# A transposed-input copy moved from VectorE to ScalarE, and a transpose round moved inside the down projection, in an eight-core transformer layer

## The chip, the cores and the metric

The kernel runs on all 8 cores of one Trainium2 chip. Each core takes one batch element of the input and runs the same program on it; the cores exchange nothing. The metric is the device time of the slowest core, in microseconds (us). The engines are called PE (TensorE), DVE (VectorE), ACT (ScalarE), POOL (GpSimd) and SP (SyncE).

## The reference

One layer with normalisation after each half, for x of 8 x 4096 x 1024, with 16 heads of 64 and a hidden width of 4096:

```python
x = _layernorm(x + attention(x, w_qkv, w_out))      # causal softmax attention
x = _layernorm(x + ffn(x, w_up, w_down))
def _ternary_linear(x, w):
    alpha = jnp.mean(jnp.abs(w))
    w_t = jnp.sign(w) * (jnp.abs(w) > 0.5 * alpha).astype(w.dtype)
    w_q = w + jax.lax.stop_gradient(w_t - w)
    rms = jnp.sqrt(jnp.sum(x * x, axis=-1, keepdims=True)) / jnp.sqrt(jnp.asarray(d, x.dtype))
    return jnp.einsum('bsd,fd->bsf', x / (rms + EPS), w_q)
# ffn: h = gelu(_ternary_linear(x, w_up)); return _ternary_linear(h, w_down)
```

## The kernel before

A core's 4096 rows of x are 32 tiles of 128 rows (NT = 32). The program has three blocks, with a barrier of all engines between them.

Phase 1 (function `phase1`) makes K and V for all tiles and sums |w_up| and |w_down| for the two thresholds. For each tile i it loads the tile as bf16 into `xb1` (POOL issues the DMA), transposes it in eight 128x128 pieces on PE into a PSUM bank (`trp` or `trq` in turn), and copies the bank to `xTs` in SBUF; that copy is the mark `xTe`. PE then transposes K of the tile before (`k_trans(i - 1)`, into `tru` or `trv`, evicted to `KT` by DVE) and runs 32 matmuls of 128x512 into `kvp`, which have to wait for `xTe`. ACT evicts the K half to `kbuf` (mark `ke`) and the V half to `VS` (mark `ve`), and then runs two passes of Abs with a sum over a 128x1024 chunk of the weights (`sqA`, mark `aact`), fed by SP's loads into `wr1`. DVE squares and reduces K for a bound of the softmax. Each engine runs its instructions strictly in the order in which the program emits them, so on ACT the two Abs passes that are emitted at the end of tile i - 1 stand ahead of everything that is emitted for tile i.

Phase 2 is the attention with the output projection and the first normalisation; x1 goes to HBM (`x1spill`). The diff doesn't touch it.

Phase 3 makes ternary weights, transposes them on PE (`tern_chunk`), and then runs the feed-forward part over the 32 tiles. For tile i, `up_trans(i)` transposes x1 on PE into the PSUM bank `tra`; DVE copies it to `x1Ts` (mark `x1Te`); the load of `x1f` is issued on SP. `up_part(i)` is 64 matmuls in 8 groups with a Gelu on ACT behind each (mark `gel`). `down_part(i)` consists of four transposing rounds `hround(0..3)`, which bring the hidden values through `trb` (rounds 0 and 2, evicted by ACT) or `tra` (rounds 1 and 3, evicted by DVE) to `hTs`, and four rounds `dround(0..3)` of 16 matmuls each into `dwn`. A handwritten order holds the loop together: `up_trans(i + 2)`, `down_part(i)`, `up_part(i + 2)`. The bank `tra` is shared by `up_trans`, `hround(1)` and `hround(3)`: `state["tra"]` keeps the mark of the eviction that has to be over before PE writes it again.

Of the kernel before, what the change touches and what calls it, by code (L numbers as in the profile page):

```python
# [10 lines left out]
AF = mybir.ActivationFunctionType  # L11
# [7 lines left out]
NT = S // 128  # L19
# [99 lines left out]
def build_program():  # L119
# [25 lines left out]
    with ExitStack() as octx:  # L145
# [38 lines left out]
        with ExitStack() as ctx:  # L184
# [6 lines left out]
            xTs = sb("xTs", [128, 2, 8, 128], BF16)  # L191
# [18 lines left out]
            def phase1(E):  # L210
                t, v, a, g, y = E.t, E.v, E.a, E.g, E.y
# [34 lines left out]
                for i in range(NT):  # L246
                    if i >= 2:
                        g.wait(("xT", i - 2))
                    E.gdma(("xb", i), xb1[:, i % 2, :],
                           x_hbm[128 * i:128 * i + 128, :])  # L250
                    t.wait(("xb", i))
                    t.wait(("c", 6))
                    if i >= 2:
                        t.wait(("xTe", i - 2))
                    xtb = (trp_b, trq_b)[i % 2]
                    for c in range(8):
                        t.transpose(xtb[:, 128 * c:128 * c + 128],
                                    xb1[:, i % 2, 128 * c:128 * c + 128],
                                    idn[:])
                    t.mark(("xT", i))  # L260
                    v.wait(("xT", i))
                    if i >= 2:
                        v.wait(("kv", i - 2))
                    v.tensor_copy(xTs[:, i % 2],
                                  xtb[:, 0:1024].rearrange(
                                      "p (c n) -> p c n", n=128))
                    v.mark(("xTe", i))
                    if i >= 1:
                        k_trans(i - 1)
                    t.wait(("xTe", i))  # L270
                    t.wait(("wkv",))
                    for nb in range(4):
                        if nb == 0 and i >= 1:
                            t.wait(("ke", i - 1))
                        if nb == 2 and i >= 1:
                            t.wait(("ve", i - 1))
                        for c in range(8):
                            t.matmul(kvp[:, 512 * nb:512 * nb + 512],
                                     xTs[:, i % 2, c, :],
                                     wkv[:, c, 512 * nb:512 * nb + 512],  # L280
                                     start=(c == 0), stop=(c == 7))
                        if nb == 1:
                            t.mark(("kvK", i))
                    t.mark(("kv", i))
                    a.wait(("kvK", i))
                    if i >= 2:
                        a.wait(("ktr", i - 2))
                        a.wait(("knr", i - 2))
                    a.activation(kbuf[:, i % 2, :], kvp[:, 0:D], AF.Copy)
                    a.mark(("ke", i))  # L290
                    a.wait(("kv", i))
                    a.wait(("vs1",))
                    a.activation(VS[:, i, :, 0:64],
                                 kvp[:, D:2 * D].rearrange(
                                     "p (h e) -> p h e", e=64), AF.Copy)
                    a.mark(("ve", i))
                    for ii in ([i - 1] if i >= 1 else []) + \
                            ([i] if i == NT - 1 else []):
                        v.wait(("ve", ii))
                        v.scalar_tensor_tensor(sqK[:], kbuf[:, ii % 2, :],  # L300
                                               1.0, kbuf[:, ii % 2, :],
                                               ALU.mult, ALU.mult)
                        v.mark(("ksq", ii))
                        v.wait(("ksq", ii))
                        v.reduce_sum(sm16[:], sqK[:].rearrange(
                            "p (h e) -> p h e", e=64), axis=AX.X)
                        v.mark(("knr", ii))
                        v.wait(("knr", ii))
                        v.wait(("km0",))
                        v.tensor_max(kmax[:], kmax[:], sm16[:])  # L310
                        v.mark(("kmx", ii))
                    for r in (2 * i, 2 * i + 1):
                        if r >= 2:
                            y.wait(("aact", r - 2))
                        if r < 32:
                            src_ap = wup_hbm[128 * r:128 * r + 128, :]
                        else:
                            rr = r - 32
                            src_ap = wdn_hbm[
                                128 * (rr // 4):128 * (rr // 4) + 128,  # L320
                                1024 * (rr % 4):1024 * (rr % 4) + 1024]
                        E.ydma(("aw", r), wr1[:, r % 2, :], src_ap)
                        a.wait(("aw", r))
                        if r >= 1:
                            a.wait(("aact", r - 1))
                        acc = (aasU[:, r:r + 1] if r < 32
                               else aasD[:, r - 32:r - 31])
                        a.activation(sqA[:], wr1[:, r % 2, :], AF.Abs,
                                     accum_out=acc)
                        a.mark(("aact", r))  # L330
# [599 lines left out]
        with ExitStack() as ctx:  # L930
# [29 lines left out]
            def phase3(E):  # L960
# [115 lines left out]
                    for q in range(8):  # L1076
                        up_part_q(i, q)

                def down_part(i):
                    def hround(k):  # L1080
                        t.wait(("gel", i, 2 * k + 1))
                        bb = (trb_b, tra_b)[k % 2]
                        if k % 2 == 0:
                            if i >= 1 or k >= 2:
                                pk = (i, k - 2) if k >= 2 else (i - 1, 2)
                                t.wait(("hTe",) + pk)
                        else:
                            t.wait(state["tra"])
                        for u in range(8):
                            t.transpose(bb[:, 128 * u:128 * u + 128],  # L1090
                                        h_sb[:, i % 2,
                                             1024 * k + 128 * u:
                                             1024 * k + 128 * u + 128],
                                        idn[:])
                        t.mark(("hT", i, k))
                        ev = a if k % 2 == 0 else v
                        ev.wait(("hT", i, k))
                        ev_src = bb[:, 0:1024].rearrange(
                            "p (c n) -> p c n", n=128)
                        if k % 2 == 0:  # L1100
                            ev.activation(hTs[:, 8 * k:8 * k + 8, :],
                                          ev_src, AF.Copy)
                        else:
                            ev.tensor_copy(hTs[:, 8 * k:8 * k + 8, :],
                                           ev_src)
                        ev.mark(("hTe", i, k))
                        if k % 2 == 1:
                            state["tra"] = ("hTe", i, k)

                    def dround(k):  # L1110
                        if k == 0 and i >= 2:
                            t.wait(("y2", i - 2))
                        t.wait(("hTe", i, k))
                        t.wait(("wTe", 32 + 8 * k + 7))
                        for fc in range(8 * k, 8 * k + 8):
                            for nb in range(2):
                                t.matmul(
                                    dwn2[i % 2][:, 512 * nb:512 * nb + 512],
                                    hTs[:, fc, :],
                                    wdnT[:, fc, 512 * nb:512 * nb + 512],  # L1120
                                    start=(fc == 0), stop=(fc == 31))

                    hround(0)
                    hround(1)
                    dround(0)
                    hround(2)
                    dround(1)
                    hround(3)
# [85 lines left out]
                for i in range(NT):  # L1214
                    if i + 3 < NT:
                        issue_x1b(i + 3)
                    if i + 2 < NT:
                        up_trans(i + 2)
                    down_part(i)
                    if i + 2 < NT:  # L1220
                        up_part(i + 2)
                y.wait(("oD", NT - 2))
# [28 lines left out]
```

How the kernel before makes its waits and increments, by code:

```python
    def mark(self, key, inc=1):  # L42
        prog = self.prog
        if prog.planning:
            prog.ctr[self.name] += inc
            assert key not in prog.marks, f"dup mark {key}"
            prog.marks[key] = (self.name, prog.ctr[self.name])
        elif self.real is not None and inc:
            self.last.then_inc(prog.sems[self.name], inc)
# [1 line left out]
    def wait(self, key):  # L51
        prog = self.prog
        if prog.planning or key is None or self.real is None:
            return
        src, val = prog.marks[key]
        seen = prog.waited.get((self.name, src), 0)
        if val <= seen:
            return
        prog.waited[(self.name, src)] = val
        self.real.wait_ge(prog.sems[src], val)
# [18 lines left out]
    def _dma(self, eng, stream, key, out, in_):  # L79
        ring = DMA_STREAMS[stream]
        if self.planning:
            o = self.snum.get(stream, 0)
            self.snum[stream] = o + 1
            sname = f"q_{stream}{o % ring}"
            assert key not in self.marks, key
            self.marks[key] = (sname, 16 * (o // ring + 1))
        if eng.real is not None:
            ins = eng.real.dma_start(out, in_)
            object.__setattr__(eng, "last", ins)
            sname, _ = self.marks[key]
            ins.then_inc(self.sems[sname], 16)
```

## Time and profile before

| what | value |
|---|---|
| median of 3 runs | 3401.02 us (3397.51 to 3469.15) |
| the profiled execution | 3402.24 us |
| its slowest core (core 7), first to last instruction | 3400.7 us |
| spans of the 8 cores | 3377.3 to 3400.7 us |
| mean granted PE clock of core 7 | 0.830 of full speed |
| PE, DVE, ACT busy | 2650.6, 971.5, 1851.8 us |

In all views "idle before <-releaser" is the time for which the engine stood still ahead of a group, and what ended it. The granted clock is given as a share of full speed (2.4 GHz); it has two levels, 1.00 and 0.50, and a number between them is a mean over a stretch. Matmuls are pipelined and the ends of their rows are modelled, so a group of matmuls reads some tenths of a us too long, and the next group can begin before it ends.

### The profile page before, as it was taken

How to read it: one execution, taken by the hardware profiler on the slowest of the kernel's cores; microseconds unless marked ns; L12 is line 12 of the kernel's file. 1: busy time of each engine (PE TensorE's matmuls, PEld its weight loads, DVE VectorE, ACT ScalarE, POOL GpSimd, SP SyncE). 2: the span in 40 equal slices, each digit the busy share in tenths (PEclk: the TensorE clock that was granted, in tenths of full speed). 3: DMA queues.
4: the chain of work that ended last, by engine and by line, in shares of the span. 5: the costliest groups of instructions: out<-in, count | busy, mean ns of one | idle time of the engine just before them, and what ended most of it. 6: DMA issues, size and time to landing. Idle time of an engine off the chain costs nothing. (4 is left out here: it accounts for less than half of the span.)

```text
span 3400.7 us, 52712 instructions; the slowest of 8 cores (3377.3 to 3400.7 us)
## 1 busy us (share of the span) xinstructions
PE 2650.6 (78%) x19808; PEld 1322.4 (39%) x19808; DVE 971.5 (29%) x2483; ACT 1851.8 (54%) x2165; POOL 115.7 (3%) x231
## 2 busy tenths in 40 slices
PE   5996466777777777787777888343699999999998
PEld 2443222333333343344344444122344444444444
DVE  5443353443332323212311201544311111111111
ACT  2553122546576877877887886445434343334343
POOL 0000000000000000000000000000000000000000
PEclk9998676777787888967889655555799999999999
DMA  6666301010101101001000000443211111111111
GB/s 134 155 156 140 49 1 50 15 51 11 50 14 33 32 1 45 20 1 38 26 1 14 26 14 1 143 136 124 71 47 45 33 47 47 38 41 47 47 32 38
DMA packets 54922, 171.26 MB, mean 50 GB/s; under 512 B 6545, under 2 KB 6546, under 8 KB 54674
## 3 DMA queue, kind: packets, MB, share of 16 engines
q1 hardware_dynamic: 37730, 134.33, 12.6%
q0 software_dynamic: 16944, 33.56, 6.8%
q8 instruction: 163, 2.67, 0.3%
q14 instruction: 85, 0.70, 0.1%
HBM read 167.87 MB, written 33.55 MB: 59 GB/s over the span
## 5 line engine op out<-in xcount | busy, mean ns | idle before, releaser
L38 ACT ACTIVATE p_sb<-sc,negC 128x1024 bf16<-128x1024 f32 (+3 forms) x1152 | 1157.9, 1041 | 505.6 <-PE pvB L38 487.9
L38 PE MATMUL sc<-QT,KT 64*128 64x512 bf16 (+3 forms) x2304 | 522.4, 446 | 180.7 <-ACT p_sb L38 177.0
L38 PE MATMUL dwn<-wdnT,hTs 128*128 128x512 bf16 x2048 | 459.9, 380 | 8.8 <-ACT hTs L38 8.8
L38 PE MATMUL upq<-wupT,x1Ts 128*128 128x512 bf16 x2048 | 454.7, 380 | 6.5 <-DVE x1Ts L38 2.0
L38 PE MATMUL pvA<-VS,p_sb 128*128 128x65 bf16 x4224 | 369.6, 213 | 33.9 <-DVE p_sb L38 19.3
L38 PE MATMUL pvB<-VS,p_sb 128*128 128x65 bf16 x4224 | 371.5, 214 | 8.3 <-DVE attO L38 8.1
L38 PEld LDWEIGHTS pvA<-VS,p_sb 128*128 128x128 bf16 x4224 | 216.8, 106 | 364.0 <-issue 359.8
L38 ACT ACTIVATE h_sb<-upq,r_all 128x512 bf16<-128x512 f32 x256 | 175.2, 685 | 228.3 <-PE upq L38 225.3
L38 PEld LDWEIGHTS upq<-wupT,x1Ts 128*128 128x128 bf16 x2048 | 198.6, 98 | 257.2 <-issue 24.4
L38 PEld LDWEIGHTS dwn<-wdnT,hTs 128*128 128x128 bf16 x2048 | 196.1, 98 | 234.3 <-issue 16.5
L38 PEld LDWEIGHTS sc<-QT,KT 64*128 64x128 bf16 x2304 | 131.6, 96 | 368.0 <-issue 338.7
L38 PEld LDWEIGHTS pvB<-VS,p_sb 128*128 128x128 bf16 x4224 | 250.2, 111 | 10.6 <-issue 10.1
L38 DVE TENSOR_TENSOR p_sb<-p_sb,tri_s 128x128 bf16<-128x128 bf16 x448 | 80.9, 222 | 605.2 <-ACT p_sb L38 602.2
L38 PE MATMUL kvp<-wkv,xTs 128*128 128x512 bf16 x1024 | 228.5, 381 | 16.5 <-DVE xTs L38 16.5
L38 PE MATMUL tra<-idn_s,wtb 128*128 128x128 bf16 x512 | 64.8, 306 | 170.4 <-DVE wtb L38 170.4
L38 PE MATMUL mmp<-xTs,wq 128*128 128x512 bf16 x512 | 178.6, 498 | 1.0 <-DVE xTs L38 1.0
L38 ACT ACTIVATE sqd<-x1f 128x1024 bf16<-128x1024 f32 x32 | 33.8, 1056 | 234.8 <-DVE x1f L38 234.8
L38 PE MATMUL mmp<-wo,aTs 128*128 128x512 bf16 x512 | 148.9, 447 | 11.8 <-DVE xfy L38 8.2
L38 PEld LDWEIGHTS kvp<-wkv,xTs 128*128 128x128 bf16 x1024 | 98.5, 98 | 136.3 <-issue 24.3
L38 ACT ACTIVATE hTs<-trb 128x1024 bf16<-128x1024 bf16 x64 | 65.5, 1024 | 153.0 <-PE trb L38 153.0
L38 ACT ACTIVATE sqd<-h_sb 128x2048 bf16<-128x2048 bf16 x64 | 122.0, 1906 | 3.2 <-ACT sqd L38 0.4
L38 DVE COPY hTs<-tra 128x1024 bf16<-128x1024 bf16 x64 | 44.3, 692 | 275.3 <-PE tra L38 275.3
(107 smaller groups left out, 1881.0 us busy)
## 6 DMA issues: line engine op xcount, KB each, us to landing
wr<-w_up SPq DMA_DIRECT2D x64, 512.0 KB, 5.2
wr<-w_down SPq DMA_DIRECT2D x64, 512.0 KB, 4.7
xb<-x POOLq DMA_DIRECT2D x64, 256.0 KB, 4.5
xfy<-x SPq DMA_DIRECT2D x32, 512.0 KB, 3.6
x1spill<-xfy SPq DMA_DIRECT2D x32, 512.0 KB, 2.6
x1f<-x1spill SPq DMA_DIRECT2D x32, 512.0 KB, 5.7
out<-outs SPq DMA_DIRECT2D x32, 512.0 KB, 6.6
x1b<-x1spill POOLq DMA_DIRECT2D x32, 256.0 KB, 3.6
```

The costliest lines, as they stand in the source:

```text
L38: getattr(self.real, op)(*args, **kw))
```

## The change

Two edits. In phase 1 the copy from the transposing bank to `xTs` is made by ACT (an activation with the function Copy) and no longer by DVE; the two waits ahead of it and the mark `xTe` behind it go with it. In phase 3 `up_trans(i + 2)` isn't called ahead of `down_part(i)` any more: `down_part` gets a parameter `mid`, a function that it calls between `dround(0)` and `hround(2)`.

```diff
@@ phase1, loop over tiles i
                     t.mark(("xT", i))
-                    v.wait(("xT", i))
+                    a.wait(("xT", i))
                     if i >= 2:
-                        v.wait(("kv", i - 2))
-                    v.tensor_copy(xTs[:, i % 2],
-                                  xtb[:, 0:1024].rearrange(
-                                      "p (c n) -> p c n", n=128))
-                    v.mark(("xTe", i))
+                        a.wait(("kv", i - 2))
+                    a.activation(xTs[:, i % 2],
+                                 xtb[:, 0:1024].rearrange(
+                                     "p (c n) -> p c n", n=128), AF.Copy)
+                    a.mark(("xTe", i))
@@ phase3
-                def down_part(i):
+                def down_part(i, mid=None):
                     def hround(k):
@@ end of down_part
                     hround(0)
                     hround(1)
                     dround(0)
+                    if mid is not None:
+                        mid()
                     hround(2)
                     dround(1)
                     hround(3)
@@ loop over tiles i
                     if i + 3 < NT:
                         issue_x1b(i + 3)
-                    if i + 2 < NT:
-                        up_trans(i + 2)
-                    down_part(i)
+                    down_part(i, mid=((lambda i2=i + 2: up_trans(i2))
+                                      if i + 2 < NT else None))
                     if i + 2 < NT:
                         up_part(i + 2)
```

## Rows read from the trace of the kernel before

**Rows 1.** Busy time by stage: us, PE, PEld, DVE, ACT, POOL; clock, DMA share, GB/s
```profile
50.40:311.60 261.20, 246.24 (x1480) 124.75 (x1480) 117.53 (x154) 130.34 (x186) 14.96 (x29) 1.00 0.67 155
...
424.00:2112.00 1688.00, 1292.23 (x12083) 642.15 (x12080) 471.26 (x1598) 1169.55 (x1270) 35.09 (x80) 0.76 0.08 22
...
2423.50:3356.00 932.50, 908.88 (x5030) 440.52 (x5028) 158.89 (x388) 375.97 (x510) 48.85 (x88) 1.00 0.17 42
```

**Rows 2.** Timeline of one tile of phase 1: start us, us, what [idle before]
```profile
158.83 0.61 PE L38 MATMUL trp<-idn_s,xb 128*128 128x128 bf16 x8
159.09 1.03 ACT L38 ACTIVATE VS<-kvp 128x1024 bf16<-128x1024 f32 x1 [2.37 <-PE kvp L38]
...
159.28 0.61 PE L38 MATMUL trv<-idn_s,kbuf 128*128 128x128 bf16 x8
159.55 0.69 DVE L38 COPY xTs<-trp 128x1024 bf16<-128x1024 bf16 x1 [4.43 <-PE trp L38]
...
160.01 1.05 ACT L38 ACTIVATE sqA<-wr 128x1024 bf16<-128x1024 f32 x1
...
160.38 7.07 PE L38 MATMUL kvp<-wkv,xTs 128*128 128x512 bf16 x32 [0.50 <-DVE xTs L38]
...
162.21 0.19 ACT L38 ACTIVATION_READ_ACCUMULATOR sqA<-wr 128x1 f32 x1
...
168.84 7.07 PE L38 MATMUL kvp<-wkv,xTs 128*128 128x512 bf16 x32 [0.50 <-DVE xTs L38]
```

**Rows 3.** What PE waited for from 48 to 314 us: total, times, longest
```profile
PE kvp L38 <- DVE xTs L38: 15.4, 31, 0.5
```

**Rows 4.** The same PSUM copy on both engines in phase 3: ns min/median/max
```profile
L38 ACT ACTIVATE hTs<-trb x60: 1016/1024/1025, 2452.8 to 3361.1; 128x1024 bf16<-128x1024 bf16 x60
L38 DVE COPY hTs<-tra x60: 691/692/693, 2453.9 to 3365.0; 128x1024 bf16<-128x1024 bf16 x60
```

**Rows 5.** Timeline, first tile of phase 1
```profile
39.66 9.39 PE L38 MATMUL kvp<-wkv,xTs 128*128 128x512 bf16 x32 [1.06 <-DVE xTs L38]
```

**Rows 6.** Timeline, last tile of phase 3, around PE's longest wait there
```profile
3371.66 0.61 PE L38 MATMUL trb<-idn_s,h_sb 128*128 128x128 bf16 x8
...
3372.10 0.61 PE L38 MATMUL tra<-idn_s,h_sb 128*128 128x128 bf16 x8
...
3375.75 5.30 PE L38 MATMUL dwn<-wdnT,hTs 128*128 128x512 bf16 x16 [3.03 <-ACT hTs L38]
```

**Rows 7.** Busy time and clock (third from the end) around that wait
```profile
3370.00:3375.70 5.70, 2.71 (x25) 1.59 (x23) 1.81 (x5) 2.15 (x4) 0.28 (x1) 1.00 0.00 1
3375.80:3379.20 3.40, 3.40 (x9) 1.22 (x10) 1.58 (x3) 0.00 (x0) 0.16 (x1) 0.50 0.32 130
3379.30:3392.00 12.70, 12.70 (x72) 6.16 (x70) 1.17 (x4) 4.92 (x5) 0.55 (x1) 1.00 0.01 3
```

**Rows 8.** The same wait on core 2, by its timeline
```profile
3360.71 5.06 PE L38 MATMUL dwn<-wdnT,hTs 128*128 128x512 bf16 x16 [3.03 <-ACT hTs L38]
```

**Rows 9.** Timeline of one tile of phase 3, from up to down
```profile
2918.67 0.61 PE L38 MATMUL tra<-idn_s,x1b 128*128 128x128 bf16 x8
...
2919.11 0.61 PE L38 MATMUL trb<-idn_s,h_sb 128*128 128x128 bf16 x8
...
2920.22 0.61 PE L38 MATMUL tra<-idn_s,h_sb 128*128 128x128 bf16 x8 [0.50 <-DVE x1Ts L38]
...
2920.99 3.61 PE L38 MATMUL dwn<-wdnT,hTs 128*128 128x512 bf16 x16 [0.16 <-ACT hTs L38]
```

**Rows 10.** Timeline of tile 30 of phase 3, where `up_trans` isn't called
```profile
3354.95 0.61 PE L38 MATMUL trb<-idn_s,h_sb 128*128 128x128 bf16 x8
...
3356.95 3.61 PE L38 MATMUL dwn<-wdnT,hTs 128*128 128x512 bf16 x16 [0.95 <-ACT hTs L38]
```

**Rows 11.** What PE waited for in phase 3, 2450 to 3370 us
```profile
PE tra L38 <- DVE x1Ts L38: 14.4, 29, 0.5
PE dwn L38 <- ACT hTs L38: 5.6, 30, 0.9
```

## The prediction

> **What bounds the kernel now.** I read the table of busy time by stage first [rows 1]. The reader is to see three stages in it. In phase 1 (50 to 312 us) PE is busy for 246.24 of 261.20 us at the full granted clock, while ACT and DVE are busy for half of the time or less: PE sets the pace. In phase 2 ACT has 1169.55 of 1688 us and PE 1292.23 at a mean clock of 0.76; the diff doesn't touch that stage. In the main part of phase 3 PE has 908.88 of 932.50 us at the full clock: PE again. So what counts is what the change adds to or takes from PE's own line of work in phases 1 and 3; work of ACT or DVE counts only where PE waits for it.
>
> The timeline of one tile of phase 1 comes next [rows 2]. PE starts the 32 matmuls of a tile at 160.38 and those of the next at 168.84, a period of 8.46 us. Between the bursts it makes two rounds of transposes (158.83 and 159.28), and then waits 0.50 us for DVE's copy `xTs`, which ran from 159.55 to 160.24. The list of PE's waits shows that this is PE's only wait in the stage: 31 times, 15.4 us in all [rows 3]. While DVE copies, ACT runs the V eviction from 159.09 and then two Abs passes, the last of which ends at 162.40 (162.21 + 0.19). Today nobody waits for that.
>
> **Phase 1 after the change.** The copy now stands in ACT's queue. ACT works its queue in the order of the program, and there V's eviction and the two Abs passes of tile i - 1 stand ahead of the copy of tile i. PE has nothing left to do in the meantime: K's transposes are issued at 159.28 and over at 159.89, and all else behind them in PE's queue is the burst that needs the copy.
> - The copy can begin when the second Abs pass has ended. The latest start is 162.40, the end of its accumulator read; if the copy overlaps that read wholly, 162.21. I take 162.35.
> - It takes 1.02 us, by the same 128x1024 bf16 copy from PSUM that ACT makes in phase 3, where DVE takes 0.69 [rows 4].
> - PE started 0.14 us after the end of DVE's copy (159.55 + 0.69 = 160.24, then 160.38) [rows 2]; ACT's hand-over is taken as the same.
> - PE starts at 162.35 + 1.02 + 0.14 = 163.51 and not at 160.38: 3.13 later, with 2.99 and 3.18 as bounds. ACT's chain starts anew at each end of a burst, so that every tile with Abs passes ahead of it pays this: tiles 1 to 31. I use 3.1, which gives 31 x 3.1 = 96 us (93 to 99). Tile 0 has nothing ahead and pays only the slower copy, 0.3 us.
>
> The weight loads into `wr1` have no part in it: they are paced by the Abs passes and get more time. DVE loses 32 x 0.69 = 22 us of work in a stage where it is busy for 45%, which is worth nothing: PE waits there for the copy alone. What is queued behind the copy on ACT is K's eviction, which needs the first half of the burst that the copy releases; it isn't late for a reason of its own.
>
> There is a rule that speaks for moving such a copy. The Trainium skill, page "VectorE: DVE Perf Modes", section "Specifications", says that VectorE sits closer to SBUF and ScalarE closer to PSUM. If a copy from PSUM were therefore no dearer on ACT, the sum would be 31 x 0.33 = 10 us smaller; the medians of 1024 against 692 ns decide against it here.
>
> **PE's clock in phase 1.** The wait makes a hole: from 159.89 to 163.51, 3.6 us in which PE stands still, once in each tile, where today the clock is 1.00 throughout. The nearest row is in the last tile of phase 3. There, too, PE comes from a burst of 32 matmuls at the full clock, makes two rounds of transposes (3371.66 and 3372.10), and stands still for 3.03 us; the burst behind it takes 5.30 us for 16 matmuls and not 3.61 [rows 6, 9], and the granted clock reads 1.00 before, 0.50 in its first 3.4 us and 1.00 after [rows 7]. The fall cost 1.69 us. The same place shows it on each of the eight cores, with 5.06 us as the lowest full row [rows 8], so a fall costs 1.45 to 1.69 us. My hole is longer than that one, so most tiles should fall. Eight of eight leaves room for a few that stay up. I take 26 of the 31 at 1.55: 40 us. The lower bound is no fall, 0 us. The upper bounds are all tiles at 1.69, 52 us, or at the price of the first tile of phase 1, which starts after a long idle time: 9.39 - 7.07 = 2.32 us [rows 2, 5], which gives 72 us.
>
> The Trainium skill, page "TensorE: Matmul & The Clock Gate", section "Why this matters for your kernels", gives the same warning: leave no long idle gaps between bursts of matmuls, or TensorE falls back to half its clock. Taken as a rule for every gap it would make all 31 fall, 48 us at 1.55.
>
> **Phase 3 after the change.** Today, counted from the end of up's last matmuls, PE issues x1's transposes at 2918.67, `hround(0)` at 2919.11, waits 0.50 for DVE's copy of x1 (the bank `tra` is shared), issues `hround(1)` at 2920.22, waits 0.16 for ACT's eviction and starts `dround(0)` at 2920.99: 2.32 us in all [rows 9]. Those waits come once a tile [rows 11]. Without `up_trans` in front, both rounds are issued at once, and `dround(0)` waits for ACT's eviction alone. Tile 30 already runs in this order, since it has no `up_trans`: from 3354.95 to 3356.95, 2.00 us, with a wait of 0.95 [rows 10]. So 0.32 us are saved. In exchange the eight transposes stand between `dround(0)` and `hround(2)`, where nothing else is idle: they take the 0.44 us that lie between the issue of x1's transposes and that of `hround(0)` (2918.67 to 2919.11) [rows 9]. The copy to `x1Ts` and the turn of the bank are covered: `hround(3)` comes after the 16 matmuls of `dround(1)` (3.61 us), against 0.69 for the copy. The load of `x1f` that `up_trans` issues on SP waits for the output of tile i, which falls in `up_part` later on, so it doesn't move, nor does what SP issues behind it; POOL's load of x1 is issued where it was. Net: 0.44 - 0.32 = +0.12 us, 30 times: +4 us. Bounds: with nothing saved, 30 x 0.44 = +13; with both waits (0.66) gone, 30 x -0.22 = -7.
>
> **Sum.** 96.4 + 40 + 4 = 140 us, on 3402.24 us of the profiled execution: 3542.6. The median of the runs is 1.2 us lower, so 3542 is the forecast, 4% slower. About 2% (68 us) is what a measurement of this kernel can tell from no change.
>
> **The rivals.**
> - *The clock holds.* The holes are real but the bursts stay at 1.00. For: phase 1's bursts are long (6.9 us), and PE ran them at 1.00 throughout. Against: rows 6 to 8. Time: 3402 + 96 + 4 = 3502.
> - *The clock costs more.* Each tile pays like the first one, 2.32 us: 3402 + 96 + 72 + 4 = 3574. If the bursts ran at half clock wholly, each would take some 6.9 us more, 214 in all: 3716. Against the latter: in rows 7 the clock is back after 3.4 us of matmuls.
> - *The copy isn't held up (the other side).* ACT would have to take it right behind V's eviction, ahead of the Abs passes, as the bank is full by then. It would end at 159.09 + 1.03 + 1.02 = 161.14, PE would start at 161.28, 0.9 us later than today, 31 x 0.9 = 28 us: 3402 + 28 + 4 = 3434, no change by 2%. It decides as soon as PE's wait grows by less than about 2 us a tile (64 / 31). The program's order speaks against it: the Abs passes are emitted first. The price would be the same if the weights' loads ran so far ahead that the passes were done early, but they wait for a free buffer and for the V eviction in the same queue.
> - *Phase 3 gains.* At best -7 us; that can't turn the sign.
>
> **How the numbers follow.** Forecast (holes, most tiles falling): 0.66, with a range of its own of 3525 to 3565. Clock holds, or falls seldom: 0.14. Clock costs more: 0.14. Copy not held up: 0.04. Something unforeseen, either side: 0.02. The range takes in the clock holding with the low bound of the copy (3402 + 93 + 4 = 3499) and the dear clock with the high bounds (3402 + 99 + 72 + 13 = 3586): 3499 to 3586. Slower by over 2%: 0.95; within 2%: 0.04; faster: 0.01.
>
> **What would show it.** In the timeline of phase 1, ACT runs V's eviction, Abs, Abs, copy in one chain without idle time, PE's wait ahead of `kvp` reads about 3.6 us and is put down to ACT's `xTs`, and the period is 11.6 us where the clock holds and about 13.2 where it fell; the burst's group reads 8.5 to 8.8 us there and 7.07 elsewhere. Phase 1's mean granted clock falls to about 0.9. In phase 3, PE's wait for `x1Ts` is gone, that for `hTs` grows to 0.95 and the period of a tile grows by 0.12 us. The forecast is wrong if PE's wait in phase 1 stays under 2 us, if the clock there reads 1.00, or if phase 3's period of a tile moves by more than 0.5 us.

## The result, and the profile after

The changed kernel takes 3535.67 us as the median of 9 runs, against 3399.85 us for the kernel before in the same comparison (10 runs), 136 us slower. The ratio is 1.0403 with a 95% interval of 1.0388 to 1.0417. The forecast was 3542 us, 140 us slower. The profiled execution took 3534.46 us; its slowest core spans 3532.9 us. Some executions of every kernel are disturbed on one die and take longer (up to 3721.22 us here); all ratios, and the times in the experiments below, go by the undisturbed ones alone (3534.5 against 3397.4 us for this pair, and only two executions for `e4_abs_behind`).

One tile of phase 1 in the timeline of the changed kernel, ACT and PE lines (start us, us, what, idle before):

```profile
163.95 0.61 PE L38 MATMUL trp<-idn_s,xb 128*128 128x128 bf16 x8
164.21 1.03 ACT L38 ACTIVATE VS<-kvp 128x1024 bf16<-128x1024 f32 x1 [2.37 <-PE kvp L38]
164.40 0.61 PE L38 MATMUL trv<-idn_s,kbuf 128*128 128x128 bf16 x8
...
165.13 1.05 ACT L38 ACTIVATE sqA<-wr 128x1024 bf16<-128x1024 f32 x1
...
166.36 1.06 ACT L38 ACTIVATE sqA<-wr 128x1024 bf16<-128x1024 f32 x1
...
167.33 0.18 ACT L38 ACTIVATION_READ_ACCUMULATOR sqA<-wr 128x1 f32 x1
167.42 1.00 ACT L38 ACTIVATE xTs<-trp 128x1024 bf16<-128x1024 bf16 x1
...
168.57 8.75 PE L38 MATMUL kvp<-wkv,xTs 128*128 128x512 bf16 x31 [3.56 <-ACT xTs L38]
```

These are the rows to set beside [rows 2]. The V eviction, the two Abs passes and the copy run on ACT as one chain; the copy begins at 167.42, beside the accumulator read of the second pass and 3.47 us after the first of x's transposes (163.95), where DVE's began 0.72 us after it. PE stands still for 3.56 us where it stood for 0.50.

The PE lines of five tiles in a row, the same view:

```profile
142.15 8.75 PE L38 MATMUL kvp<-wkv,xTs 128*128 128x512 bf16 x31 [3.56 <-ACT xTs L38]
155.36 8.75 PE L38 MATMUL kvp<-wkv,xTs 128*128 128x512 bf16 x31 [3.56 <-ACT xTs L38]
168.57 8.75 PE L38 MATMUL kvp<-wkv,xTs 128*128 128x512 bf16 x31 [3.56 <-ACT xTs L38]
181.77 7.07 PE L38 MATMUL kvp<-wkv,xTs 128*128 128x512 bf16 x31 [3.56 <-ACT xTs L38]
193.29 8.75 PE L38 MATMUL kvp<-wkv,xTs 128*128 128x512 bf16 x31 [3.56 <-ACT xTs L38]
```

(One record of the 32 is missing in each of these groups.) A burst here is the group of 32 matmuls of one tile, and the hole is the time for which PE stands still ahead of it. The hole is the same each time, but the burst is 8.75 us long or 7.07. After a burst of 7.07 the next tile starts 11.52 us later (181.77 to 193.29), after one of 8.75, 13.21 us later. In the whole stage 8 of the 31 bursts behind a hole keep their 7.07 us; the other 23 are longer by about 1.69 us (some of their groups are split, or read 0.2 us less, where a record is missing). Two stretches inside such a burst, in the table of busy time by window (the clock is third from the end):

```profile
169.60:173.00 3.40, 3.40 (x9) 1.21 (x8) 0.00 (x0) 0.00 (x0) 0.00 (x0) 0.50 0.87 213
173.10:181.70 8.60, 5.06 (x35) 2.70 (x34) 3.17 (x4) 5.14 (x7) 0.53 (x1) 1.00 0.23 22
```

For 3.4 us the granted clock is at the lower of its two levels, 1.2 GHz, as in [rows 7]; 3.4 us at half speed are 1.7 us of work lost, which is the 1.69 by which the group is longer. In these tiles the fall doesn't come while PE stands still. The same table for the hole ahead of the burst at 193.29, and for the first 2 us of this burst and of the next three:

```profile
189.80:193.20 3.40, 0.00 (x0) 0.00 (x0) 3.15 (x4) 3.26 (x6) 0.53 (x1) 1.00 0.57 98
193.30:195.30 2.00, 2.00 (x6) 0.78 (x7) 0.00 (x0) 0.00 (x0) 0.00 (x0) 0.55 0.81 240
206.50:208.50 2.00, 2.00 (x7) 0.80 (x8) 0.00 (x0) 0.00 (x0) 0.00 (x0) 0.67 1.04 216
219.70:221.70 2.00, 2.00 (x8) 0.86 (x9) 0.00 (x0) 0.00 (x0) 0.00 (x0) 0.78 1.09 328
232.90:234.90 2.00, 1.99 (x10) 0.94 (x11) 0.00 (x0) 0.00 (x0) 0.00 (x0) 1.00 0.96 248
```

The clock reads 1.00 through the hole and on into the burst. A mean of 0.55 over 2 us, full first and half after, is 0.2 us at full clock (1.0 x 0.2 + 0.5 x 1.8 = 1.1 = 0.55 x 2) and so a fall 0.2 us after the burst has begun; in the next two bursts it comes 0.7 and 1.1 us after, and in the fourth there is none.

What PE waited for from 48 to 440 us, against [rows 3], and the stages, against [rows 1]:

```profile
PE kvp L38 <- ACT xTs L38: 111.1, 31, 3.9
```

```profile
50.40:440.00 389.60, 277.29 (x1423) 132.12 (x1453) 98.63 (x123) 156.45 (x214) 14.81 (x28) 0.90 0.44 104
440.00:2270.00 1830.00, 1328.66 (x12315) 670.11 (x12395) 514.83 (x1700) 1183.49 (x1295) 44.41 (x98) 0.76 0.10 25
2590.00:3480.00 890.00, 849.99 (x4689) 417.97 (x4774) 153.44 (x375) 353.72 (x484) 47.32 (x85) 1.00 0.16 42
```

PE's waits in phase 1 went from 15.4 to 111.1 us, and phase 1's clock from 1.00 to 0.90. The clock of phase 2 is 0.76 in both kernels.

The length of phase 1 is best read from the tile view of `kvp`, whose line gives the first and the last start of the 512-column matmuls. Before, and after:

```profile
L38 PE MATMUL kvp<-wkv,xTs x1024: 376/379/631, 39.7 to 310.8; 128*128 128x512 bf16 x171
```

```profile
L38 PE MATMUL kvp<-wkv,xTs x994: 376/379/634, 39.2 to 444.1; 128*128 128x512 bf16 x199
```

271.1 us became 404.9: +133.8, nearly all of the loss.

Phase 3, from up to down, in the timeline after, against [rows 9]:

```profile
3018.35 0.61 PE L38 MATMUL trb<-idn_s,h_sb 128*128 128x128 bf16 x8
...
3018.80 0.61 PE L38 MATMUL tra<-idn_s,h_sb 128*128 128x128 bf16 x8
3019.20 1.02 ACT L38 ACTIVATE hTs<-trb 128x1024 bf16<-128x1024 bf16 x1
...
3020.57 3.40 PE L38 MATMUL dwn<-wdnT,hTs 128*128 128x512 bf16 x15 [1.17 <-ACT hTs L38]
3023.81 0.61 PE L38 MATMUL tra<-idn_s,x1b 128*128 128x128 bf16 x8
3024.26 0.61 PE L38 MATMUL trb<-idn_s,h_sb 128*128 128x128 bf16 x8
```

The first matmul of the `dwn` group has no record here (15 of 16), so the wait reads 1.17; with the 0.22 us of one matmul taken off it is 0.95, as in [rows 10]. The wait for `x1Ts` is gone from PE's list (2590 to 3490 us), where [rows 11] had both:

```profile
PE dwn L38 <- ACT hTs L38: 33.8, 29, 1.2
```

From the end of up to the start of down it is 2.0 us, and x1's transposes, now inside down, take 0.45 of PE (3023.81 to 3024.26). The period of a tile went from 31.14 to 31.27 us.

### The profile page after: what moved, and what is told of

Its sections match the earlier page's. It is cut to its first block and busy times, and to the rows that moved or that the text cites. A ratio compares the mean times of both kernels' runs of the same rounds, so it can differ in the third digit from the quotient of the medians.

```text
span 3532.9 us, 52503 instructions; the slowest of 8 cores (3519.1 to 3532.9 us)
## 1 busy us (share of the span) xinstructions
PE 2648.6 (75%) x19600; PEld 1331.5 (38%) x19808; DVE 952.3 (27%) x2451; ACT 1881.4 (53%) x2197; POOL 116.0 (3%) x231
## 5 line engine op out<-in xcount | busy, mean ns | idle before, releaser
L38 PE MATMUL dwn<-wdnT,hTs 128*128 128x512 bf16 x1984 | 446.6, 380 | 40.4 <-ACT hTs L38 38.5
L38 PE MATMUL kvp<-wkv,xTs 128*128 128x512 bf16 x994 | 264.1, 427 | 115.0 <-ACT xTs L38 112.5
L38 PEld LDWEIGHTS kvp<-wkv,xTs 128*128 128x128 bf16 x1024 | 108.2, 108 | 260.7 <-issue 171.6
L38 PE MATMUL mmp<-xTs,wq 128*128 128x512 bf16 x461 | 162.5, 495 | 10.4 <-issue 7.4
L38 PE MATMUL mmp<-wo,aTs 128*128 128x512 bf16 x482 | 135.8, 434 | 18.2 <-DVE xfy L38 8.3
```

Source lines behind the costliest of these rows:

```text
L38: getattr(self.real, op)(*args, **kw))
```

## The experiments

All are built on one of the two kernels. The theory that they test has two parts. The queue: the copy costs what it costs because it stands behind two Abs passes in ACT's queue, and PE can't fill the time. The clock: part of the loss is no waiting at all, but matmuls at half clock behind the hole. The rivals are that ACT as the engine of this copy is the cause, that the rest beyond the waiting comes from somewhere else, and that the phase 3 edit has a larger share.

**Each edit alone.** `e1_copy_only` has the first hunk of the diff and the old phase 3, `e2_mid_only` the other hunks and DVE's copy.

> Only the copy to xTs moves to ACT; phase 3 as before. If nearly all of the loss is phase 1 (31 waits of 3.1 us and some 23 to 26 falls of the clock at 1.5 to 1.7 us), the time is 3400 + 132 = 3532 us, within 5. If the phase 3 edit cost a third of the loss or more, it would be under 3490.

> Only up_trans moves into down_part; the copy stays on DVE. By the working from tile 30 it costs 30 x 0.12 to 0.14 = 4 us: 3404. If the two waits that it removes were worth their whole 0.66 us a tile it would be 7 us faster, 3393; if nothing were saved, 13 us slower, 3413.

Measured: `e1_copy_only` 3533.84 us, ratio 1.0407 (1.0390 to 1.0423); `e2_mid_only` 3399.90 us, ratio 1.0004 (0.9990 to 1.0018). The copy is nearly the whole loss. The tile view of `dwn` shows the second edit as small but there: from the first to the last down matmul it is 969.8 us before and 973.8 us in `e2_mid_only`.

```profile
L38 PE MATMUL dwn<-wdnT,hTs x2048: 376/379/634, 2422.1 to 3391.9; 128*128 128x512 bf16 x187
```

```profile
L38 PE MATMUL dwn<-wdnT,hTs x1984: 377/379/631, 2416.8 to 3390.6; 128*128 128x512 bf16 x199
```

The 4.0 us are the forecast's, and so is the period of a tile, 31.27 us for 31.14 (30 x 0.13 = 3.9). The two lines are of different cores; over all eight the length is 968.7 to 969.8 us before and 971.6 to 974.4 in `e2_mid_only`, for the burst of the last tile is slow on some cores and not on others. In the total the interval allows for -3 to +6 us and can't tell them from nothing.

**The clock by itself.** `e3_fill` is the changed kernel with work of no use in the hole: matmuls of the weights with themselves into the transposing bank that is idle, overwritten later.

```diff
                         k_trans(i - 1)
+                    if i >= 1:
+                        fb = (trp, trq)[(i + 1) % 2]
+                        for c in range(12):
+                            t.matmul(fb[:, 0:512],
+                                     wkv[:, c % 8, 0:128],
+                                     wkv[:, c % 8, 0:512],
+                                     start=True, stop=True)
+                        t.mark(("fill", i))
                     t.wait(("xTe", i))
```

> The changed kernel with 12 matmuls of 128x512 into an idle PSUM bank in each tile from 1 on, issued behind K's transposes, where PE stands still for 3.6 us; their results are overwritten. They take 12 x 0.216 = 2.6 us of the hole. If the clock's falls cost what lies above the 96 us of waiting, the bursts read 7.07 us throughout, the clock of phase 1 reads 1.00 and the time falls by 23 x 1.69 = 39 us to some 3500. If the rest came from somewhere else, the time stays at 3536 or rises.

Measured: 3497.75 us, ratio 1.0322 (1.0270 to 1.0374). With 12 matmuls more in each of 31 tiles the kernel is 37 us faster than the changed one (3534.5). The interval is wide, because one of the four executions took 3529.92 us, but it doesn't touch the changed kernel's (1.0388 to 1.0417); the price itself is read from the stage. Its timeline, the windows from 52 to 300 us, and the tile view of `kvp`:

```profile
154.41 2.54 PE L38 MATMUL trq<-wkv 128*128 128x512 bf16 x11
...
156.77 1.00 ACT L38 ACTIVATE xTs<-trp 128x1024 bf16<-128x1024 bf16 x1
157.92 7.07 PE L38 MATMUL kvp<-wkv,xTs 128*128 128x512 bf16 x32 [0.97 <-ACT xTs L38]
```

```profile
52.00:300.00 248.00, 225.21 (x1262) 109.35 (x1281) 69.25 (x87) 109.89 (x151) 11.15 (x21) 1.00 0.44 117
```

```profile
L38 PE MATMUL kvp<-wkv,xTs x1024: 376/379/631, 40.0 to 406.5; 128*128 128x512 bf16 x171
```

The burst still starts no earlier, for it waits for the same copy, but it reads 7.07 us and the clock 1.00. Phase 1 is 366.5 us long, 38.4 less than after (38.0 to 39.4, core by core), and no burst of it behind a hole is slow on any core. The clock's share is thus measured: 38.4 us, against 23 x 1.69 = 38.9 from the bursts' lengths. The rest, 366.5 - 271.1 = 95.4 us, is waiting.

**The place in the queue.** In `e4_abs_behind` and `e5_one_abs_ahead` the copy stays on ACT, but the Abs passes of tile i - 1 are emitted behind the copy of tile i, both or only the second; phase 3 is the old one. The body of the loop over the passes is made a function `abs_pass(r)`. The edit of `e4_abs_behind`, against the changed kernel:

```diff
                     a.mark(("xTe", i))
+                    if i >= 1:
+                        abs_pass(2 * (i - 1))
+                        abs_pass(2 * (i - 1) + 1)
...
-                    for r in (2 * i, 2 * i + 1):
...
```

> Copy to xTs on ACT as in the changed kernel, but the two Abs passes of tile i - 1 are emitted behind the copy of tile i; phase 3 as before. If the place in ACT's queue is the cause, PE waits 1.4 us a tile and not 3.56, 0.9 us more than before, and the clock stays up: 3400 + 28 = 3428. If the cause were ACT itself as the engine of this copy, the time would stay near 3530.

> Copy on ACT, with one of the two Abs passes of tile i - 1 left ahead of it and the other behind; phase 3 as before. By the queue, PE waits about 2.3 to 2.5 us a tile, 31 x 1.9 to 2.0 = 61 us more than before. For the clock the hole is between the one of 1.4 us that cost nothing and the one of 3.56 us that made about 23 of 31 tiles fall: 0 to 23 falls of 1.69 us, so 3461 to 3500, with falls in about half as many tiles as the likeliest, 3480.

Measured: `e4_abs_behind` 3425 us, 26 us above the 3399 of the kernel before; `e5_one_abs_ahead` 3457.85 us, ratio 1.0161 (1.0107 to 1.0214). The waits of PE in `e4_abs_behind` and then in `e5_one_abs_ahead`, both from 52 to 300 us:

```profile
PE kvp L38 <- ACT xTs L38: 33.8, 26, 1.6
```

```profile
PE kvp L38 <- ACT xTs L38: 53.9, 23, 2.6
```

1.3 us a tile with no pass ahead, 2.3 with one, 3.6 with two: each pass that stands ahead adds 1.0 to 1.2 us, about the time of one pass with its accumulator read (165.13 to 166.36 in the timeline above). The engine is the same in all three. For the clock, the expectation of `e5_one_abs_ahead` missed. It took the likeliest case to be half as many falls as after, 3480 us. The time lies 3 us under the lower end of what was given, 3461, and the timeline shows a single burst of 8.75 us in the stage; all others behind a hole are short:

```profile
61.66 7.07 PE L38 MATMUL kvp<-wkv,xTs 128*128 128x512 bf16 x31 [2.32 <-ACT xTs L38]
71.94 8.75 PE L38 MATMUL kvp<-wkv,xTs 128*128 128x512 bf16 x31 [2.32 <-ACT xTs L38]
84.22 7.07 PE L38 MATMUL kvp<-wkv,xTs 128*128 128x512 bf16 x31 [2.63 <-ACT xTs L38]
```

So 31 holes of 1.3 us made no burst slow, 31 of 2.3 us made one slow, and 31 of 3.56 us made 23 slow. These counts are the same on each of the eight cores; the single slow burst of `e5_one_abs_ahead` is another tile's on most of them. The cost of the clock doesn't grow in step with the hole.

**The same copy, early enough.** In `e6_early_dve` and `e7_early_act` PE transposes tile i + 1 ahead of the last quarter of tile i's burst, and the copy is emitted behind K's eviction; on DVE in the one, on ACT in the other. Phase 3 is the old one.

```diff
                         if nb == 0 and i >= 1:
                             t.wait(("ke", i - 1))
+                        if nb == 3 and i + 1 < NT:
+                            x_trans(i + 1)
...
                     a.mark(("ke", i))
+                    if i + 1 < NT:
+                        x_copy(i + 1)
```

> Phase 1 only: PE transposes tile i + 1 ahead of the last quarter of tile i's burst, and DVE's copy is made meanwhile; phase 3 as before. PE's waits of 0.50 us go away, 31 x 0.5 = 15 us: 3385. If the copy's engine matters more than its place, this and the next run differ.

> The same early transposes with the copy on ACT, behind K's eviction. If the place in the queue is all, ACT's slower copy (1.02 against 0.69 us) is hidden like DVE's and the time is 3385 as well, 150 us below the changed kernel although the copy is on the same engine. If ACT as such is the cause, it stays above 3400 by 10 us or far more.

Measured: 3375.46 us on DVE, ratio 0.9933 (0.9902 to 0.9964), and 3379.16 us on ACT, ratio 0.9941 (0.9913 to 0.9968). The tile views of `kvp`, DVE and then ACT:

```profile
L38 PE MATMUL kvp<-wkv,xTs x1024: 379/379/631, 39.6 to 289.5; 128*128 128x512 bf16 x171
```

```profile
L38 PE MATMUL kvp<-wkv,xTs x1024: 379/379/631, 39.9 to 291.0; 128*128 128x512 bf16 x171
```

249.9 and 251.1 us: the stage takes the same time on either engine (249.9 to 251.3 and 249.8 to 251.2 over the eight cores). On ACT it is 154 us less than in the changed kernel, with the very same instruction on the very same engine. That rules out the engine as the cause. Both are 20 to 21 us shorter than before, 0.66 us a tile, not the 15 us expected. The wait that was read as 0.50 us stood for more: the row of the transposes at 159.28 [rows 2] reads 0.61 us, while from one such round to the next it is 0.45 (158.83 to 159.28), and 0.16 us of waiting are hidden in it.

**Phase 3 with the wait covered.** `e8_early_h0` has the phase 3 edit and DVE's old copy; `hround(0)` of the next tile is issued ahead of the last of up's eight groups, so that ACT's eviction runs under 1.7 us of matmuls.

```diff
                     if i + 2 < NT:
-                        up_part(i + 2)
+                        for q in range(7):
+                            up_part_q(i + 2, q)
+                    if i + 1 < NT:
+                        hround(i + 1, 0)
+                    if i + 2 < NT:
+                        up_part_q(i + 2, 7)
```

> Phase 3 only: up_trans inside down_part as in the changed kernel, and hround(0) of the next tile issued ahead of the last of up's eight groups; phase 1 as before. PE's wait for hTs (0.95 to 1.17 us a tile) is covered by 1.7 us of matmuls: about 30 x 0.8 = 24 us less than with up_trans moved alone, some 3378. If the wait only turned into one for the Gelu evictions, it stays at 3400.

Measured: 3365.07 us, ratio 0.9888 (0.9845 to 0.9931). From the first to the last down matmul:

```profile
L38 PE MATMUL dwn<-wdnT,hTs x2048: 379/379/634, 2411.9 to 3354.6; 128*128 128x512 bf16 x187
```

942.7 us, 31.1 less than in `e2_mid_only`. The core shown is the longest of the eight (939.0 to 942.7): the burst of its last tile is slow and reads 6.57 us. The period of a tile is 30.16 us and was 31.27 in `e2_mid_only`, 1.1 a tile; the expectation of 0.8 was low, and the time lies 13 us under the 3378 given. PE's list of waits from 2500 to 3300 us has one line left:

```profile
PE upq L38 <- ACT h_sb L38: 0.5, 1, 0.5
```

Moving `up_trans` pays only in this order. That it takes both is argued and not shown: had `up_trans` stayed in front of down, `hround(1)` would still wait for DVE's copy of x1, but no run has the early `hround(0)` with `up_trans` in its old place.

**Both together.** `e9_both` joins `e6_early_dve` and `e8_early_h0`, `e10_both_act` is the same with ACT's copy.

> The early transposes of phase 1 with the copy on DVE and the early hround(0) of phase 3 together. The two stages don't overlap, so the gains add up: 271 to 250.6 us in phase 1 and 34 us in phase 3, some 3345 us. If one of them were given back elsewhere (in phase 2's clock, say) it would stay at 3365.

> The same with the copy on ACT, as both edits of the change have it: 3345 us too, within 5, if the engine of the copy is worth nothing once the copy is early enough. If ACT's copy costs something after all, it is 10 us or more slower.

Measured: 3346.91 us, ratio 0.9856 (0.9838 to 0.9874), and 3348.32 us, ratio 0.9855 (0.9838 to 0.9873). By stage the gains add up: in `e9_both` phase 1 takes 251.1 us and phase 3, from the first to the last down matmul, 942.4. By the ratios the two single gains come to 1.8% (0.7 and 1.1) and the joint one to 1.4%, a difference that the intervals allow for. The engine of the copy makes no difference, and the kernel is 1.4% faster than the one before and 5% faster than the changed one.

## Why the prediction was right

- **What bounds the stages.** PE's own line of work was the measure in phases 1 and 3, and phase 2 didn't react (clock 0.76 in both kernels).
- **The copy behind the Abs passes.** The forecast put PE's start 3.1 us later a tile, with the copy beginning near the end of the second accumulator read. It begins 0.09 us after that read starts (167.42 against 167.33), earlier than the point taken, and takes 1.00 us, so the growth of the wait is 3.06 us (3.56 - 0.50), inside the bounds of 2.99 and 3.18. In all it is 95.4 us, measured by `e3_fill`, against 96.4 forecast.
- **The clock.** The price of a fall was taken as 1.55 us from the bounds of 1.45 and 1.69, the number as 26 of 31. It is 1.69 in nearly all and 23: 38.4 us against 40, two small errors against each other, and that they cancel is luck. The one place in the trace of before that had the shape of the new hole [rows 6 to 8] foretold the price well. The number it couldn't foretell, and "eight of eight" meant less than it seemed. The same hole of 3.03 us stands ahead of the last tile's down in the other kernels too, behind the same kinds of work, and it made the burst slow on 7 of 8 cores in the changed kernel, on 6 in `e2_mid_only`, on 3 in `e8_early_h0` and on 2 in `e9_both`. A spared one (core 7 of the changed kernel), and the dearest (core 5 of `e8_early_h0`), which took 2.96 us more than that, where the forecast read 1.69 as the upper price from this place:

```profile
3507.89 3.61 PE L38 MATMUL dwn<-wdnT,hTs 128*128 128x512 bf16 x16 [3.04 <-ACT hTs L38]
```

```profile
3337.19 6.57 PE L38 MATMUL dwn<-wdnT,hTs 128*128 128x512 bf16 x16 [3.03 <-ACT hTs L38]
```

- **What stays open.** The runs don't say why about three tiles in four are hit and the fourth is not. They show that the length of the hole alone doesn't decide it. The forecast's reason for most tiles falling, that the hole is longer than the one of the last tile, is thus only in part a reason, and the 26 was a guess that came near.
- **The two rules cited.** The Trainium skill, page "TensorE: Matmul & The Clock Gate", section "Why this matters for your kernels", warns of idle gaps between bursts. The runs agree in kind; taken for every gap it is too strict, with 8 of 31 spared at 3.56 us. The placement that the Trainium skill, page "VectorE: DVE Perf Modes", section "Specifications", gives for ScalarE made no copy from PSUM cheaper: 1.00 to 1.02 us on ACT, 0.69 on DVE.
- **Phase 3.** +4 us forecast, +4.0 from first to last down matmul and +0.13 us a tile, where the forecast had 0.12. Tile 30 of the kernel before, which already ran in the new order, was the right row to read.
- **The rivals.** The clock that holds would have given 3502 us; `e3_fill`, which makes it hold, gives 3498. The copy that isn't held up was put at 3434 us, 3430 with the old phase 3; `e4_abs_behind`, which has the old one, gives 3425. Both are real kernels, but neither is this change: the order in the program decides.

## What to carry to other kernels

Before an operation moves to another engine, look not at that engine's busy share but at what stands ahead in its queue at the moment when the result is wanted: ACT was busy for half of phase 1, and still the copy came 3 us late, while the same copy on the same engine was free once it was emitted at a moment when ACT was idle. A new stall of TensorE has two prices, the waiting and the clock: look in the trace for a place where it already stands still for about as long, and read the burst behind it. That gives the price of a slow burst; how many there will be it doesn't give. And a tile at the edge of a loop, where a step is left out, often shows the order that a change would bring.

## What was not expected of the hardware

The clock's fall is far from proportional to the wait. At holes of 1.3, 2.3 and 3.56 us, 0, 1 and 23 of 31 bursts were slow, on each of the eight cores, and each slow one of phase 1 lost up to 1.69 us, at 2.3 us as at 3.56. On the core shown of the changed kernel the fall comes not in the hole but behind it, 0.1 to 1.3 us after the burst has begun, and later from each slow burst to the next until one is spared. The pattern is regular, mostly three slow ones and one at full speed, in 51.1 us (181.77 to 232.91 from one fast burst to the next). And work of no use can pay: 12 matmuls a tile whose results are never used took 38 us off phase 1.
